# Recommender kernel: TensorE's fills in threes, two accumulator banks in turn, gathers paced one by one

## The chip, the cores and the metric

The kernel runs on one core of one Trainium2 chip. The metric is device time in microseconds. TensorE's granted clock is given as a share of 2.4 GHz; it stands at 1.00 in all windows of the steady part.

## The reference

An xDeepFM over 2048 samples, 26 sparse fields with embeddings of 32 numbers, 13 dense features, all in float32:

```
emb = tables[feat_idx, sparse]                       # 2048 x 26 x 32
linear_out = lin_sparse_w[feat_idx, sparse].sum(-1) + dense @ lin_dense_w
x0 = xk = emb; res = []
for w, bb in ((conv1_w, conv1_b), (conv2_w, conv2_b)):
    hp = einsum('bhd,bmd->bhmd', xk, x0).reshape(-1, h * 26, 32)
    xn = sigmoid(einsum('oi,bid->bod', w, hp) + bb)  # 128 outputs
    xk = xn[:, :64]; res.append(xn[:, 64:])
cin_out = concat(res).sum(-1) @ cin_w + cin_b
h1, h2, h3 = three tanh layers of 1024, 512, 256 on [emb, dense]
result = linear_out + cin_out + h3 @ deep_w + deep_b + bias
```

## The kernel before

The batch is cut into 16 tiles of 128 samples. A tile is worked on in 4 steps of 8 embedding dimensions, so that a step has 8 x 128 = 1024 columns; there are 64 steps. Tile 0, tiles 1 to 13 (a hardware loop), tile 14 and tile 15 are four copies of one program (`over_tiles`; `ahead` is 3, 2, 1, 0). After them the three dense layers run over 4 groups of 512 samples.

In one step:

- **First layer.** TensorE writes sums of two fields into PSUM (K fills, `spread_sum`, L738, 3 of 2 matmuls each), ScalarE squares them (L922) into `sq`, and TensorE contracts `sq` with weights (`contract_k`, L745) in two chunks of 512 columns. Both chunks use the one bank `xn`. ScalarE reads each chunk with three sigmoids (`read_xn`, L926 to L928) and so makes `xk` of the next step.
- **Second layer.** 13 products, number n = 0 to 12: VectorE multiplies the rows of two fields, spread over 128 partitions, with `xk` (L692). For 7 of the 13 (`BY_DMA`) two DMAs of 256 KB each copy the field's rows from DRAM into a buffer `xb` (SyncE, L471). For 6 (`BY_PE`) TensorE spreads them into PSUM (`spread_pair`, L731); the six take three slots of PSUM (`bc`) in turn together with the K fills. One spread is two matmuls of 32 rows, on row groups that depend on `group_of(n)`. TensorE contracts each product into bank `y2` (L751, 4 matmul records for a product, two at a time on the two halves of the columns), and ScalarE reads it (L932).
- **Next tile.** GpSimd gathers 26 rows for each sample with 26 indirect DMAs (L542). In one step of a tile (`deep_step`: step 1, in tile 0 step 2) TensorE turns the gathered tile (D fills, L723), ScalarE copies it twice (L918, L919), VectorE takes the remainder (`lower_deep`, L658), and SyncE dumps both to DRAM (`dump`, L420; `dump_halves`, L433), from where `x0t` is loaded on ScalarE's queue (`load_rows`, L370).
- GpSimd also adds up what ScalarE has read (`add_up`, L553 to L558).

`STEP_WORK` is the order on TensorE, and ScalarE follows it: "of_last" are products of the step before, "of_this" those of this step, "first" is a chunk of the first layer. VectorE takes the products in order of n. SyncE loads `xb` again once TensorE has contracted it.

Of the kernel before, what the change touches and what calls it, by code (L numbers as in the profile page):

```python
# [41 lines left out]
def second_of_pair(p):  # L42
# [12 lines left out]
ORDER = [0, 1, 2, 3, 8, 4, 5, 9, 6, 7, 10, 11, 12]  # L55
BY_PE = (3, 4, 6, 7, 9, 10)
# [8 lines left out]
    ("of_last", (8, 9, 10)),  # L65
    ("fill", (("D", 0), ("D", 1), ("D", 2))),
    ("of_last", (11, 12)),
    ("fill", (3, 4)),
    ("first", 0),
    ("of_this", (0, 1, 2)),  # L70
    ("fill", (6, 7)),
    ("first", 1),
    ("fill", (9, 10)),
    ("of_this", (3, 4, 5, 6, 7)),
# [40 lines left out]
assert all(group_of(BY_PE[i]) != group_of(BY_PE[i + 1]) for i in range(0, len(BY_PE), 2))  # L115
# [17 lines left out]

AHEAD = 5, 12, 19
assert AHEAD[-1] <= M

# [19 lines left out]
def build(nc, table, sparse, dense_t, lin_dense, pair_a, pair_b, diag_ab, w2rows, conv1_b, conv2_b,  # L158
          cin_w, scalars, W1, b1, W2, b2, W3, b3, deep_w, select, ident_f, out):
    with ExitStack() as ctx:  # L160
# [81 lines left out]
        xn = pb("xn", [P, CHUNK])  # L242
        y2 = pb("y2", [P, CHUNK])
# [78 lines left out]
        def k_contracted_by(s, c):  # L322
            return s * 2 + (2 + c + 1)

# [51 lines left out]
        def _(sp):  # L376
# [96 lines left out]
            def tile(t, is_first, ahead):  # L473
                for sl in range(STEPS):
                    s = t * STEPS + sl
                    for i, n in enumerate(BY_DMA):
                        if not (is_first and sl == 0):
                            sp.wait_ge(contracted, contracted_by(s - 1, n))
                            hold()
                        spread_by_dma(t, sl, i)  # L480
                        if i == 2 and sl == 2 and not is_first and ahead > 0:
                            dump_halves(t + 1)
                    if sl == 2 and is_first:
                        dump_halves(t + 1)
                    if sl == deep_step(ahead) and ahead > 0:
                        dump(t + 1)
                    if sl == STEPS - 1 and ahead == 0:
                        sp.wait_ge(dense_dumped, 64)
                        load_x(0, 0, 1)
# [36 lines left out]
        def _(pool):  # L526
# [43 lines left out]

            def tile(t, is_first, ahead):
                s = t * STEPS
                if is_first:
                    free_emb(t, DEEP_N)
                    gather(range(PAIRS), gathered)
                else:
                    if ahead > 0:
                        gather(range(AHEAD[2], AHEAD[2] + 3), gathered)
                    add_up(t - 1, STEPS - 1, r2, r2_step, y2_read, 1, sum2)
                    if ahead > 0:  # L580
                        gather(range(AHEAD[2] + 3, M), gathered)
                add_up(t, 1, r1, r1_step, xn_read, 2, sum1)
                if is_first:
                    gather(range(PAIRS, M), gathered)
                elif ahead > 1:
                    free_emb(t + 1, filled_by(t, 1, ("D", DEEP_N - 1), ahead))
                    gather(range(AHEAD[0]), gathered)
                add_up(t, 2, r1, r1_step, xn_read, 2, sum1)
                if is_first:
                    add_up(t, 1, r2, r2_step, y2_read, 1, sum2)  # L590
                    free_emb(t + 1, filled_by(t, 2, ("D", DEEP_N - 1), ahead))
                    gather(range(9), gathered)
                else:
                    if ahead > 1:
                        gather(range(AHEAD[0], AHEAD[0] + 3), gathered)
                    add_up(t, 1, r2, r2_step, y2_read, 1, sum2)
                    if ahead > 1:
                        gather(range(AHEAD[0] + 3, AHEAD[1]), gathered)
                add_up(t, 3, r1, r1_step, xn_read, 2, sum1)
                if is_first:  # L600
                    gather(range(9, 13), gathered)
                elif ahead > 1:
                    gather(range(AHEAD[1], AHEAD[1] + 3), gathered)
                add_up(t, 2, r2, r2_step, y2_read, 1, sum2)
                if is_first:
                    gather(range(13, AHEAD[2]), gathered)
                elif ahead > 1:
                    gather(range(AHEAD[1] + 3, AHEAD[2]), gathered)
# [5 lines left out]
        def _(dve):  # L614
# [61 lines left out]
            def tile(t, is_first, ahead):  # L676
                for sl in range(STEPS):
                    s = t * STEPS + sl
                    start = is_first and sl == 0
                    for n in range(PAIRS):  # L680
                        if n == 0:
# [11 lines left out]
                        if n == 3 and sl == deep_step(ahead) and ahead > 0:  # L693
                            dve.wait_ge(gathered, t * GATHERED + GATHERED)
                            sum_linear(t + 1)
                        if n == 5 and sl == deep_step(ahead) and ahead > 0:
                            dve.wait_ge(deep_rounded, t * DEEP_N + 2 * DEEP_N)
                            for ks in DEEP_PARTS:
                                lower_deep(ks)
# [18 lines left out]
        def _(pe):  # L718
# [23 lines left out]
            def contract_k(c):  # L742
                cols = slice(c * CHUNK, (c + 1) * CHUNK)
                for k in range(K1):
                    last = nc.tensor.matmul(xn[:, :], w1s[:, k, :], sq[k][:, cols], start=(k == 0), stop=(k == K1 - 1))  # L745
                last.then_inc(k_contracted, 1)

            def contract(n):
                src = product(n)
                for c in range(2):  # L750
                    last = nc.tensor.matmul(y2[H * c:H * c + H, :], w2s[:, ORDER[n], :], src[:, c * CHUNK:(c + 1) * CHUNK],  # L751
# [43 lines left out]
            contract_k(0)  # L795
            pe.wait_ge(xn_read, 1)
            contract_k(1)
# [3 lines left out]
            def add_term(w, x, start=False, stop=False):  # L801
                for g in range(GROUPS):
                    last = nc.tensor.matmul(xn[32 * g:32 * g + 1, 0:CHUNK], w, x[:, g * CHUNK:(g + 1) * CHUNK],
# [3 lines left out]
            def add_linear():  # L807
                for c in range(CHUNK // P):
                    for g in range(GROUPS):
                        t = g * (CHUNK // P) + c  # L810
                        nc.tensor.matmul(xn[32 * g:32 * g + 1, c * P:(c + 1) * P], lin_sum[:, t:t + 1], idf[:, :],
                                         start=False, stop=False, skip_group_check=True)

            def tile(t, is_first, ahead):
                for sl in range(STEPS):
# [4 lines left out]
                    for kind, what in STEP_WORK:  # L820
# [268 lines left out]
```

## Time and profile before

| | |
|---|---|
| median of 3 runs | 1616.76 us (1615.88 to 1619.33) |
| the profiled execution's own time | 1624.22 us |
| its span | 1622.4 us |
| TensorE, share of the span | 95% |
| VectorE / ScalarE / GpSimd | 68% / 40% / 44% |
| DMA queue of SyncE / ScalarE / GpSimd | 75.0% / 4.1% / 3.8% of 16 engines |

A line of the profile gives an engine's busy time, the number of instructions, and, in the chain of waits, what released each piece of work. "Idle before" is the time an engine had nothing to do before a group, with the work that ended it. Step 0 of a tile is the first of its four.

### The profile page before, as it was taken

The numbers are of one execution on the slowest core, as the hardware profiler recorded it, in microseconds if no ns is written. First come the engines' busy times: TensorE is split into PE (matmuls) and PEld (weight loads), VectorE is DVE, ScalarE is ACT, GpSimd is POOL, SyncE is SP. The second block draws the span as 40 slices with busy tenths as digits, with TensorE's granted clock in tenths as the row PEclk, the third lists the DMA queues.
The fourth block names the chain that finished last, engine by engine and source line by source line (L and its number), as shares of the span: only waits on it lengthen the run. The fifth ranks groups of instructions, "written<-read, shape, count | busy, mean of one in ns | idle before, by whom it ended". The sixth has DMA issues, their size and how long they took to land.

```text
span 1622.4 us, 23599 instructions
## 1 busy us (share of the span) xinstructions
PE 1543.6 (95%) x6584; PEld 656.8 (40%) x6584; DVE 1104.7 (68%) x1017; ACT 643.5 (40%) x904; POOL 709.2 (44%) x600
## 2 busy tenths in 40 slices
PE   0598999999999999999999999999999999999999
PEld 0232333333333333333333333333333336787876
DVE  3276777777777877787777777787877783333332
ACT  2342434344434443434443434434343323344443
POOL 7356565556555556565555646464731110000000
PEclk9899999999999999999999999999999999999999
DMA  6688999999999999999998989898999884634531
GB/s 126 143 183 194 231 214 223 217 231 209 226 212 225 211 224 209 221 214 229 210 228 200 232 201 231 201 240 201 237 203 235 204 210 122 186 120 147 175 104 53
DMA packets 178599, 319.80 MB, mean 197 GB/s; under 512 B 31132, under 2 KB 106812, under 8 KB 178524
## 3 DMA queue, kind: packets, MB, share of 16 engines
q1 hardware_dynamic: 155423, 298.87, 75.0%
q10 hardware_dynamic: 9828, 13.43, 4.1%
q0 software_dynamic: 13312, 7.06, 3.8%
q8 instruction: 19, 0.31, 0.1%
q14 instruction: 17, 0.14, 0.0%
HBM read 297.93 MB, written 21.31 MB: 197 GB/s over the span
## 4 chain that ended last, share of the span: by engine, by line
PE 86%; issue 4%; DVE 3%; another core or an unknown queue 2%; POOL 2%; DMA 1%; SPq 1%; ACT 1%; ACTq 0%; DVEq 0%; POOLq 0%
PE y L751 42%; PE xn L745 19%; PE bc L880 16%; PE bc L731 5%; PE bc L738 3%; DVE hp L692 2%; POOL emb L542 2%; PE bc L723 1%; DVE xb L692 1%; SPq L465 1%; DMA x0t<-x_halves 1%; DMA x_lo<-dense_halves 0%; ACTq L370 0%; DMA emb<-table,idx_stage 0%
## 5 line engine op out<-in xcount | busy, mean ns | idle before, releaser
L692 DVE TENSOR_TENSOR hp<-bc,xk 128x1024 f32<-128x1024 f32 x384 | 453.9, 1219 | 271.3 <-PE bc L731 136.0
L542 POOL DMA_INDIRECT emb<-table,idx_stage x416 | 515.9, 1240 | 145.5 <-issue 126.3
L692 DVE TENSOR_TENSOR xb<-xb,xk 128x1024 f32<-128x1024 f32 x448 | 546.5, 1264 | 27.9 <-ACT xk L927 23.9
L751 PE MATMUL y<-xb,w2s 128*64 128x512 f32 x1792 | 436.0, 601 | 0.0
L745 PE MATMUL xn<-sq,w1s 128*128 128x512 f32 x768 | 369.7, 618 | 4.4 <-issue 4.4
L751 PE MATMUL y<-hp,w2s 128*64 128x512 f32 x1536 | 366.0, 597 | 0.0
L553 POOL TENSOR_TENSOR r<-r 128x512 f32<-128x512 f32 x96 | 123.5, 1287 | 351.0 <-ACT r L932 181.3
L926 ACT ACTIVATE xk<-xn,bias 64x512 f32<-64x512 f32 x128 | 87.4, 683 | 438.5 <-PE xn L745 248.8
L922 ACT ACTIVATE sq<-bc 128x1024 f32<-128x1024 f32 x192 | 182.9, 1026 | 197.5 <-PE bc L738 145.8
L751 PEld LDWEIGHTS y<-xb,w2s 128*64 128x64 f32 x1792 | 116.0, 136 | 248.8 <-issue 201.5
L745 PEld LDWEIGHTS xn<-sq,w1s 128*128 128x128 f32 x768 | 137.5, 192 | 162.6 <-issue 154.8
L751 PEld LDWEIGHTS y<-hp,w2s 128*64 128x64 f32 x1536 | 104.8, 137 | 199.5 <-issue 172.4
L713 DVE TENSOR_TENSOR h_lo<-h_raw,h_hi 128x512 fp32r<-128x512 f32 x48 | 33.2, 692 | 154.2 <-ACT h_hi L1021 154.2
L731 PE MATMUL bc<-x0t,sel 32*128 32x512 f32 x768 | 97.2, 496 | 6.8 <-DVE hp L692 3.5
L731 PEld LDWEIGHTS bc<-x0t,sel 32*128 32x128 f32 x768 | 36.8, 182 | 158.1 <-issue 122.0
L932 ACT ACTIVATE r<-y,bias 128x512 f32<-128x512 f32 x64 | 44.0, 687 | 127.4 <-PE y L751 127.4
L880 PE MATMUL bc<-x_hi,w_hi 128*128 128x512 f32 (+1 forms) x224 | 88.4, 395 | 3.6 <-DMA x_lo<-dense_halves 2.8
L1019 ACT ACTIVATE h_raw<-bc,bd 128x512 f32<-128x512 f32 x48 | 33.0, 688 | 142.7 <-PE bc L880 142.7
L928 ACT ACTIVATE r<-xn,bias 64x512 f32<-64x512 f32 x128 | 87.5, 684 | 3.2
L880 PE MATMUL bc<-x_lo,w_hi 128*128 128x512 f32 (+1 forms) x224 | 88.2, 394 | 0.0
L880 PE MATMUL bc<-x_hi,w_lo 128*128 128x512 f32 (+1 forms) x224 | 88.1, 394 | 0.0
L927 ACT ACTIVATE xk<-xn,bias 64x512 f32<-64x512 f32 x128 | 87.2, 681 | 1.7
(57 smaller groups left out, 843.3 us busy)
## 6 DMA issues: line engine op xcount, KB each, us to landing
xb<-x_rows SPq DMA_DIRECT2D x896, 256.0 KB
w_raw<-W SPq DMA_DIRECT2D x32, 448.0 KB
x0t<-x_halves ACTq DMA_DIRECT2D x252, 52.0 KB
x_halves<-deep_halves SPq DMA_DIRECT2D x30, 384.0 KB
w_raw<-W SPq DMA_DIRECT2D x16, 512.0 KB
emb<-table,idx_stage POOLq DMA_INDIRECT x416
x_hi<-x_halves SPq DMA_DIRECT2D x24, 256.0 KB
x_lo<-x_halves SPq DMA_DIRECT2D x24, 256.0 KB
```

The lines of the kernel that those rows point to most:

```text
L542: nc.gpsimd.indirect_dma_start(out=emb[:, m, :], out_offset=None, in_=table, in_offset=bass.IndirectOffsetOnAxis(ap=idx_stage[:, m:m + 1], ...
L553: nc.gpsimd.tensor_tensor(total, r[:, 0, :] if sl == 1 else total, r[:, sl, :], ALU.add).then_inc(step, 1)
L692: nc.vector.tensor_tensor(product(n)[:, :], x[:, :], xk[sl % 2][:, :], ALU.mult).then_inc(multiplied, 1)
L731: last = nc.tensor.matmul(bc[slot][:, c * CHUNK:(c + 1) * CHUNK], sel[rows, ORDER[n], :], x[rows, :], start=True, stop=True)
L738: last = nc.tensor.matmul(bc[slot][:, c * CHUNK:(c + 1) * CHUNK], sel[rows, PAIRS + k, :], x[rows, :], start=True, stop=True)
L745: last = nc.tensor.matmul(xn[:, :], w1s[:, k, :], sq[k][:, cols], start=(k == 0), stop=(k == K1 - 1))
L751: last = nc.tensor.matmul(y2[H * c:H * c + H, :], w2s[:, ORDER[n], :], src[:, c * CHUNK:(c + 1) * CHUNK], start=(n == 0), stop=(n == PAIRS ...
L880: last = nc.tensor.matmul(bc[a % 2][:, 0:CHUNK], w[a % 2][part, k, :], x[part, at, :], start=(k == 0 and i == 0), stop=(k == rows - 1 and ...
L922: nc.scalar.activation(sq[k][:, :], bc[slot][:, :], ACT.Square).then_inc(squared, 1)
L926: nc.scalar.activation(xk[slot][0:H, cols], xn[0:H, :], ACT.Sigmoid, bias=bias1[0:H, :])
L927: nc.scalar.activation(xk[slot][H:P, cols], xn[0:H, :], ACT.Sigmoid, bias=bias1[0:H, :]).then_inc(xk_made, 1)
L928: nc.scalar.activation(r1[H * c:H * c + H, sl, :], xn[H:P, :], ACT.Sigmoid, bias=bias1[H:P, :]).then_inc(xn_read, 1)
```

## The change

1. `ORDER` and `BY_PE`: TensorE spreads products 0, 1, 2 and 5, 6, 7, in two fills of three; 3, 4 and 8 to 12 are copied by DMA.
2. `STEP_WORK`: products 5 to 12 are contracted a step later, 0 to 4 in their own step. The two chunks of the first layer stand next to each other. The last step has an order of its own (`FINAL_WORK`).
3. Two banks `acc` take turns: chunk c of step sl goes to `acc[(sl + c) % 2]`, the products to `acc[sl % 2]`.
4. Each gather waits until a named product is multiplied (`gather_in`).
5. VectorE does the tile's sum and remainders ahead of product 0 instead of behind products 3 and 5.
6. SyncE dumps the halves right before the rows, and the inputs of the first dense group are loaded in steps of tiles 14 and 15 instead of at the end.

```diff
-ORDER = [0, 1, 2, 3, 8, 4, 5, 9, 6, 7, 10, 11, 12]
-BY_PE = (3, 4, 6, 7, 9, 10)
+ORDER = [0, 8, 1, 3, 4, 9, 2, 10, 5, 6, 7, 11, 12]
+BY_PE = (0, 1, 2, 5, 6, 7)
...
+FINAL_WORK = (
+    ("fill", (0, 1, 2)),
+    ("of_last", (5, 6, 7, 8, 9, 10, 11, 12)),
+    ("fill", (5, 6, 7)),
+    ("of_this", (0, 1)),
+    ("terms", None),
+    ("of_this", (2, 3, 4)),
+)
...
-        xn = pb("xn", [P, CHUNK])
-        y2 = pb("y2", [P, CHUNK])
+        acc = [pb(f"acc{i}", [P, CHUNK]) for i in range(2)]
+        terms = acc[(STEPS - 2) % 2]
...
+        def first_acc(sl, c):
+            return acc[(sl + c) % 2]
...
-                        if i == 2 and sl == 2 and not is_first and ahead > 0:
-                            dump_halves(t + 1)
-                    if sl == 2 and is_first:
+                    if sl == deep_step(ahead) and ahead > 0:
                         dump_halves(t + 1)
-                    if sl == deep_step(ahead) and ahead > 0:
                         dump(t + 1)
-                    if sl == STEPS - 1 and ahead == 0:
-                        sp.wait_ge(dense_dumped, 64)
-                        load_x(0, 0, 1)
+                    if ahead == 1:
+                        if sl == 0:
+                            sp.wait_ge(dense_dumped, 64)
+                        load_x(0, sl, 4 * STEPS)
+                    if ahead == 0 and sl < STEPS - 1:
+                        load_x(0, 1 + sl, STEPS)
...
+            def gather_in(s, fields, ns):
+                for m, n in zip(fields, ns):
+                    pool.wait_ge(multiplied, multiplied_by(s, n))
+                    hold()
+                    gather((m,), gathered)
...
+                if ahead > 0:
+                    gather_in(s - 1, range(20, 23), (8, 10, 12))
+                add_up(t - 1, STEPS - 1, r2, r2_step, y2_read, 1, sum2)
+                if ahead > 0:
+                    gather_in(s, range(23, M), (2, 4, 6))
+                add_up(t, 1, r1, r1_step, xn_read, 2, sum1)
...
                     for n in range(PAIRS):
+                        if n == 0 and sl == deep_step(ahead) and ahead > 0:
+                            dve.wait_ge(gathered, t * GATHERED + GATHERED)
+                            sum_linear(t + 1)
+                            for i, ks in enumerate(DEEP_PARTS):
+                                dve.wait_ge(deep_rounded, t * DEEP_N + (DEEP_N + i + 1))
+                                lower_deep(ks)
...
                             for use in uses:
-                                if is_product(use):
+                                if not is_d(use):
                                     slot_free(t, sl, use, is_first, ahead)
...
                         elif kind == "of_this":
-                            if what[0] == 0 and not start:
-                                pe.wait_ge(y2_read, s)
+                            if what[0] == 0:
+                                pe.wait_ge(xn_read, s * 2 + (2 if final else 3))
...
                         elif kind == "first" and not final:
                             if what == 0:
                                 pe.wait_ge(squared, squared_by(s, K1 - 1))
-                            pe.wait_ge(xn_read, s * 2 + (2 + what))
-                            contract_k(what)
+                            if what == 0:
+                                pe.wait_ge(xn_read, s * 2 + 2)
+                            elif not start:
+                                pe.wait_ge(y2_read, s)
+                            contract_k(what, first_acc(sl, what))
```

What TensorE runs in one step, from the K fills of a step on, before the change (`bc` are the three slots, `x0t` the rows, `hp` and `xb` the products, a K fill has `L738`, a spread `L731`; a product has 2 matmuls here):

```order
L738 MATMUL bc<-x0t,sel 128x512 x6
L751 MATMUL y<-xb,w2s 64x512 x2
L751 MATMUL y<-hp,w2s 64x512 x4
L751 MATMUL y<-xb,w2s 64x512 x4
L731 MATMUL bc<-x0t,sel 128x512 x4
L745 MATMUL xn<-sq,w1s 128x512 x3
L751 MATMUL y<-xb,w2s 64x512 x6
L731 MATMUL bc<-x0t,sel 128x512 x4
L745 MATMUL xn<-sq,w1s 128x512 x3
L731 MATMUL bc<-x0t,sel 128x512 x4
L751 MATMUL y<-hp,w2s 64x512 x4
```

and the same place after it:

```order
L755 MATMUL bc<-x0t,sel 128x512 x6
L768 MATMUL acc<-hp,w2s 64x512 x6
L768 MATMUL acc<-xb,w2s 64x512 x10
L748 MATMUL bc<-x0t,sel 128x512 x6
L762 MATMUL acc<-sq,w1s 128x512 x6
L748 MATMUL bc<-x0t,sel 128x512 x6
L768 MATMUL acc<-hp,w2s 64x512 x6
L768 MATMUL acc<-xb,w2s 64x512 x4
```

The two chunks of the first layer moved together, the spreads went from three blocks of two to two blocks of three, and eight products of the step before stand in a row behind the K fills where there were five.

GpSimd at the start of the loop's tile, before (each DMA is the gather of one field):

```order
L542 DMA emb<-table,idx_stage 128x33 x3
L553 TENSOR_TENSOR r<-r 128x512 [waits r2_step]
L556 TENSOR_TENSOR r<-r 128x256 [waits r2_step]
L558 TENSOR_TENSOR sum<-r 128x128
L542 DMA emb<-table,idx_stage 128x33 x4
```

and after, where tile 14 has the same order without the register work:

```order
L550 DMA emb<-table,idx_stage 128x33 [waits multiplied] x3
L561 TENSOR_TENSOR r2<-r2 128x512 [waits r2_step,y2_read]
L564 TENSOR_TENSOR r2<-r2 128x256 [waits r2_step]
L566 TENSOR_TENSOR sum2<-r2 128x128 [waits r2_step]
L550 DMA emb<-table,idx_stage 128x33 [waits multiplied] x3
```

Each gather has got a wait for VectorE, and the last of the 26 (the third of the lower group) waits for product 6 of step 0.

## Rows read from the trace of the kernel before

**Rows 1.** The page, busy time of each engine.
```profile
PE 1543.6 (95%) x6584; PEld 656.8 (40%) x6584; DVE 1104.7 (68%) x1017; ACT 643.5 (40%) x904; POOL 709.2 (44%) x600
```

**Rows 2.** Chain of waits, 231 to 272 us: start, length, work.
```profile
231.83 4.44 PE y L751 x20
236.28 0.89 PE bc L738 x3
237.16 4.45 PE y L751 x20
241.61 0.44 PE bc L731 x3
242.05 2.77 PE xn L745 x6
244.82 2.73 PE y L751 x12
...
251.20 4.44 PE y L751 x20
...
259.26 0.92 PE bc L723 x7
...
271.61 0.58 PE y L751
```

**Rows 3.** TensorE in order of time: start, length, line, tiles, idle time before.
```profile
136.19 1.65 PE L738 MATMUL bc<-x0t,sel 64*128 64x512 f32 x6 [7.42 <-DMA x0t<-x_halves]
...
1302.61 0.97 PE L738 MATMUL bc<-x0t,sel 64*128 64x512 f32 x6
...
1321.88 1.03 PE L751 MATMUL y<-xb,w2s 128*64 128x512 f32 x4
...
1342.01 1.89 PE L751 MATMUL y<-xb,w2s 128*64 128x512 f32 x8
1346.70 0.47 PE L880 MATMUL bc<-x_hi,w_hi 128*128 128x512 f32 x1 [2.80 <-DMA x_lo<-dense_halves]
```

**Rows 4.** VectorE in order of time, same step as rows 2.
```profile
242.20 2.35 DVE L692 TENSOR_TENSOR hp<-bc,xk 128x1024 f32<-128x1024 f32 x2 [2.01 <-PE bc L731]
```

**Rows 5.** ScalarE in order of time, same step (ACTq: DMAs it issues).
```profile
241.81 3.58 ACTq L370 DMA_DIRECT2D x0t<-x_halves  x4
245.58 0.68 ACT L926 ACTIVATE xk<-xn,bias 64x512 f32<-64x512 f32 x1 [3.23 <-PE xn L745]
246.28 0.68 ACT L927 ACTIVATE xk<-xn,bias 64x512 f32<-64x512 f32 x1
246.99 0.68 ACT L928 ACTIVATE r<-xn,bias 64x512 f32<-64x512 f32 x1
```

**Rows 6.** GpSimd, a gather at 611.55 us, and GpSimd's DMA queue from 614.5 to 615.4.
```profile
611.55 1.70 POOL L542 DMA_INDIRECT emb<-table,idx_stage  x1 [0.22 <-issue]
...
q0 software_dynamic: 31, 0.02, 20.4%
```

**Rows 7.** GpSimd, a tile's last gather, its DMA queue from 413.5 to 414.3, TensorE's D fills.
```profile
406.92 0.95 POOL L542 DMA_INDIRECT emb<-table,idx_stage  x1 [0.31 <-issue]
...
q0 software_dynamic: 2, 0.00, 0.8%
...
416.19 0.98 PE L723 MATMUL bc<-idf,emb 128*128 128x128 f32 x7
```

**Rows 8.** ScalarE's DMA issues at 597.45 us, and its DMA queue from 601.2 to 606.
```profile
597.45 3.58 ACTq L370 DMA_DIRECT2D x0t<-x_halves  x4
...
q10 hardware_dynamic: 156, 0.21, 22.2%
```

**Rows 9.** Busy time by stretch, 400 to 600 us; last: TensorE's clock, DMA share, GB/s.
```profile
400.00:600.00 200.00, 198.97 (x846) 68.86 (x844) 157.26 (x145) 82.27 (x118) 112.32 (x94) 1.00 0.95 220
```

**Rows 10.** Tile 0, SyncE's dump of the halves and ScalarE's load behind it.
```profile
120.04 0.99 SPq L433 DMA_DIRECT2D x_halves<-deep_halves  x2
...
125.25 3.20 ACTq L370 DMA_DIRECT2D x0t<-x_halves  x4
```

**Rows 11.** VectorE, the remainder of the second dense weights.
```profile
1348.47 1.09 DVE L664 TENSOR_TENSOR w_lo<-w_raw,w_hi 128x896 fp32r<-128x896 f32 x1 [8.29 <-ACT w_hi L909]
```

## Prediction before the run

> **What bounds the kernel now.** I read the page first: TensorE is busy for 95% of the span, VectorE for 68%, and nothing else over half [rows 1]. Then the chain of waits over two steps of a middle tile. It holds nothing but TensorE: blocks that follow each other without a gap, 19.37 us from one block of products (231.83) to the same block a step later (251.20), and 20.41 us (251.20 to 271.61) in the step that turns the next tile [rows 2]. So TensorE's own order is the bound, and the reader should see two things in it. First, a block costs more than its matmuls: products take 4.44 us for 20 records and 2.73 for 12 [rows 2], so a record costs (4.44 - 2.73) / 8 = 0.214 us and a block 0.165 us on top. The first layer's records run one at a time where the products' run in twos, so I take 2 x 0.214 = 0.428 for one; six make 2.57, and the block's 2.77 leaves 0.20. Second, waits are rare: from the K fills of tile 0's step 3 (136.19) to those of tile 15's step 2 (1302.61) are 59 steps, 14 of them with D fills, and 1166.4 us [rows 3]. Without any wait they would be 59 x 19.37 + 14 x 1.04 = 1157.4. So 9 us are waits and a slow restart at 136.
>
> **The steps, summed.** Before, a step is three blocks of products (4.44, 4.45, 2.73), K fills 0.89, three fills of two spreads at 0.44, two blocks of the first layer at 2.77 [rows 2]: 19.37. After, it is K fills 0.89, products 5 to 12 in one block (32 records: 0.165 + 32 x 0.214 = 7.01), two fills of three spreads, one block of the first layer (12 x 0.428 + 0.20 = 5.34), products 0 to 4 (4.44). The one unknown is the fill of three spreads. Their groups alternate: two can run on different rows of the array, the third needs the rows of the first. The rows give 0.44 for one round (two spreads) and 0.89 for three rounds (K fills, which use all rows each) [rows 2], so a further round costs (0.89 - 0.44) / 2 = 0.225, and three spreads are two rounds: 0.665. The ends are 0.44 (all at once) and 0.89 (each alone). With 0.665 the step is 0.89 + 7.01 + 0.665 + 5.34 + 0.665 + 4.44 = 19.01, which is 0.36 less. Over 59 steps: -21.2. At the ends: -48 and +5. I take the middle, since the groups are known. In a D step the D fills cut the block of products in two, before and after alike, so the 1.04 stays.
> The Trainium skill (TensorE: Matmul & The Clock Gate, Part 3, The mechanism) says that a weight load runs beside a matmul in flight only when the row group differs. By that rule the third spread waits for the first, as in the 0.665. Were its weights kept waiting for the whole array, the fill would be the 0.89 and the step 19.46.
>
> **Do the others keep up?** I walk through a step, with 0 as the start of the fill of 0, 1, 2 (B). VectorE starts 0.6 after such a fill begins and then makes a product every 1.13 us (2.35 for two) [rows 4]: products 0 to 4 end at 1.8, 3.0, 4.1, 5.2, 6.4. TensorE's first layer ends at 6.0, and its fill of 5, 6, 7 needs the slots of 0, 1, 2, free at 4.1: no wait. Product 5 ends at 7.9, 6 at 9.0, 7 at 10.1, 12 at 15.8. TensorE contracts 0 to 4 from 6.7 to 11.1. The K fills, which now wait for product 7 (10.1), start at 11.1; product 12 is needed at 18.1. ScalarE issues four loads from 0.2 on and starts to read chunk 0 at 4.0, as it does now (245.58 against 241.61), done at 6.1 [rows 2, 5]; TensorE needs that bank at 6.7. This wait, which is new, has the least room, 0.5 us. Behind it stand all contractions of the step. Chunk 1 is read from 6.1 to 8.2, far before the next step needs `xk`. ScalarE's squares end at 14.9, needed at 19. So none of the new waits should end last, and 5 of the 9 us of waits before go, since slots are free 0.9 to 1.9 us ahead; the other 4 (the restart mostly) stay. Ends: 0 and -9.
>
> **DMA.** The engines are busy for 0.95 of a stretch of steps at 220 GB/s [rows 9]; the bytes stay and the steps get 2% shorter, which asks for 224. The copies' room grows: product 3's buffer is asked for at -8.9 and needed at 5.2; that of 8 at -3.4, needed at 11.2; that of 12 at about 2.4 (SyncE issues one behind the other), needed at 14.7. The loads of `x0t` lose room: issued until 3.8, they are needed at 11.1, where before it was 255.64, 14.0 after B. In the rows all their packets fall before 606, within 5.0 us of the last issue's end (601.03) [rows 8]; 7.3 are left. I take 0.
> The Trainium skill (DMA: Bandwidth & Descriptors, Queues, rings and completion order) says that a DMA engine goes round its queues packet by packet, so that these loads don't stand behind five queued copies. The row with 156 packets of ScalarE's queue amid SyncE's agrees; in a strict order of issue they would come some 4 us later and just in time. Neither changes the sum.
>
> **The gathers.** The last one now waits for product 6 of step 0, at 9.0, and is issued at 9.15. The D fills stand at 11.1 + 0.9 + 2.7 = 14.7. That leaves 5.5 us where a last gather now has 9.3 (406.92 to 416.19) [rows 7]. How long does one take? From its start to its packets' end 3.8 us for one after a pause [rows 6], 7.2 for the last of a burst (406.92 to after 413.5, a few packets) [rows 7], and some time more until it is counted, which no row shows. So TensorE waits 0 to 2 us for each of 14 tiles: 0 to +28. Paced gathers are nearer to the first row; I take 0.45 each: +6. With that wait VectorE's remainder and the dumps move too, but they have 2 us of room.
>
> **Tile 0.** Step 3 waits for the load of `x0t` behind the dump: dump at 120.04, load at 125.25, K fills at 136.19 after 7.4 us idle [rows 3, 10]. The remainders now stand ahead of product 0, so the dump can leave earlier, but the load is needed earlier too and the chain (10.9 us from load to fills) remains; it sets when tile 1 starts, so what the prologue saves is lost in it. I take -2, ends -6 and +4.
>
> **The end.** The last step has three more products to contract than before (8 of the old step instead of 5), of which the step before had fewer: 23.3 us from its first block to its end (0.67 fills + 7.0 + 0.6 wait for product 2 + 0.67 + 1.8 + terms 2.9 + 2.7 + 6.9), against 21.8 (1321.88 to 1342.01 + 8 x 0.214 = 1343.7) [rows 3]: +1.5. The dense layers' input is there by then: the 3.0 us from 1343.7 to 1346.70 shrink to 0.3 [rows 3], but the second dense product, 5.1 us behind, needs weights that come 5.8 us after the end (1349.56) [rows 11], through ScalarE, which waits for GpSimd's last sums: -2.7 + 0.7 = -2.0. The loads of 4 MB now lie in the steps of tile 15, 1 MB each, where gathers and dumps are absent; I cost them at 0, and up to +4 if the copies fall behind.
>
> **Sum.** -21.2 - 5 + 6 - 2 + 1.5 - 2.0 = -22.7 us. The profiled execution took 1624.22, so 1601.5; it lay 7.5 above the median of 1616.76, from which the forecast is counted: **1594 us**.
>
> **Rivals.**
> 1. *Gathers land late (slower).* Place: TensorE before the D fills. Saved without this term: 28.7 us; over 14 tiles that is gone at a wait of 2.05 us each, thus at 7.6 us from the gather's start to its count. At 9.3 us, the most that the trace allows (it never waited), the wait is 3.8 x 14 = 53 and the time 1641. For it: 7.2 in rows 7, and DMA at 0.95. Against it: 3.8 in rows 6, and the burst is gone. Typical of it: 1630.
> 2. *A fill of three costs what the K fills cost.* Step 19.46: +0.45 x 59 = 26.5 over the forecast, 1620. For it: nothing in the trace shows three spreads. Against: two go at once at 0.44.
> 3. *DMA can't go faster.* If 220 GB/s is its limit, a step falls behind the copies and stays near 19.3: 1610. For it: the share of 0.95. Against: TensorE does not wait for copies now [rows 2].
> 4. *All waits go.* No gather wait, all 9 us go: 1584.
> 5. *The turn of banks or the adjacent chunks make ScalarE's read the last* (0.5 us of room missed by 0.3): +18, 1612.
>
> **Chances.** Forecast 0.56, rival 1 0.08, rival 2 0.06, rival 3 0.08, rival 4 0.15, rival 5 0.07. The range that holds 8 in 10 takes in rivals 4, 3 and part of 5: 1580 to 1612. A difference under 0.2% (3.2 us) can't be told from none here. Faster by more than that: forecast, 4, 3, 5 and little else, 0.85; same 0.05 (rival 2 in part); slower 0.10.
>
> **What would show it.** Right: in the chain of waits a step of 19.0 us with blocks of 32 and 20 records; a fill of three at 0.66 to 0.67; the first layer in one block of 5.3. K to K over the same 59 steps near 1142. Wrong: fills of 0.89; TensorE idle before its D fills for gathers by more than 1 us a tile, or before the first product of a step for ScalarE's reads of the first layer's bank; a share of DMA at 1.0 with VectorE waiting for `xb`; the time from the last product to the first dense matmul still near 3.

## The result: slower by half a per cent

| | before | changed |
|---|---|---|
| median, us (lowest to highest, 16 runs each, one chip) | 1617.62 (1613.85 to 1619.61) | 1625.80 (1616.50 to 1632.06) |
| ratio, 95% interval | | 1.0051 (1.0040 to 1.0063) |
| profiled execution: its time, its span | 1624.22, 1622.4 | 1626.34, 1624.5 |

A second measurement on another chip gave 1626.18 against 1616.67, ratio 1.0062 (1.0046 to 1.0077). Forecast were 1594 us and a range of 1580 to 1612: the sign is wrong and the range missed.

The changed kernel's page, busy time by engine, the chain's shares by engine, and the groups of the K fills and of VectorE's products from copies:
```profile
PE 1523.4 (94%) x6584; PEld 669.6 (41%) x6584; DVE 1125.6 (69%) x1017; ACT 643.7 (40%) x904; POOL 679.7 (42%) x600
...
PE 61%; DMA 25%; ACTq 7%; issue 3%; POOL 2%; ACT 1%; SPq 1%; DVE 0%; POOLq 0%; DVEq 0%
...
L716 DVE TENSOR_TENSOR xb<-xb,xk 128x1024 f32<-128x1024 f32 x448 | 563.1, 1314 | 3.4 <-DMA xb<-x_rows 3.3
...
L755 PE MATMUL bc<-x0t,sel 64*128 64x512 f32 x384 | 63.8, 437 | 48.3 <-DMA x0t<-x_halves 38.9
```
TensorE is busy for 20.2 us less than before [rows 1] and the span is no shorter: the saving is there and has been handed back as waiting. Who is waited for stands in the second and the last line: a quarter of the chain is DMA, and the K fills sat idle for 48.3 us, mostly for the loads of `x0t`.

The chain of waits over two steps of the stretch of [rows 2], changed kernel (start, length, what):
```profile
225.68 8.43 DMA x0t<-x_halves
...
234.15 0.96 PE bc L755 x6
235.12 7.02 PE acc L768 x32
242.13 0.66 PE bc L748 x6
242.79 5.35 PE acc L762 x12
248.14 0.66 PE bc L748 x6
248.80 4.44 PE acc L768 x20
253.25 0.89 PE bc L755 x6
254.14 2.73 PE acc L768 x12
256.86 0.92 PE bc L740 x7
257.78 4.44 PE acc L768 x20
```
Two things are to be seen. Where nothing is late, a step is 0.89 + 7.02 + 0.66 + 5.35 + 0.66 + 4.44 = 19.02 us, against 19.01 forecast, and each block is within 0.01 of its term. And in front of it stands a load that took 8.43 us from the start of its issue (225.68) until TensorE could go on, 7.66 from the issue's end (226.45). The waits, first in the whole run, then from 180 to 1300 us (who <- for whom: us, times, longest):
```profile
PE bc L755 <- DMA x0t<-x_halves: 38.9, 41, 8.6
```
```profile
PE bc L755 <- DMA x0t<-x_halves: 29.1, 38, 2.2
```
Outside tile 0 they are short, 0.8 us on average (29.1 / 38), but two steps in three have one. TensorE's own rows, beside [rows 3]:
```profile
130.09 1.65 PE L755 MATMUL bc<-x0t,sel 64*128 64x512 f32 x6 [8.62 <-DMA x0t<-x_halves]
...
213.14 1.62 PE L755 MATMUL bc<-x0t,sel 64*128 64x512 f32 x6 [2.22 <-DMA x0t<-x_halves]
...
1304.71 0.96 PE L755 MATMUL bc<-x0t,sel 64*128 64x512 f32 x6
...
1346.71 1.08 PE L768 MATMUL acc<-xb,w2s 128*64 128x512 f32 x4 [0.16 <-DVE xb L716]
1347.72 0.50 PE L899 MATMUL bc<-x_hi,w_hi 128*128 128x512 f32 x1
```
The 59 steps take 1304.71 - 130.09 = 1174.6 us, where [rows 3] give 1166.4. By its blocks they should take 59 x 19.02 + 14 x 1.04 = 1136.7. Of the 37.9 that are left, 29.5 are listed as waits for loads (38.9 without the two in tile 0, 8.6 and 0.7). Some 4.0 are slower matmuls behind the two longest waits: the K fills at 213.14, after 2.22 us idle, took 1.62 where those at 1304.71 took 0.96, and the step from 130.09 lasted until 151.41, 2.3 us over its blocks without a wait in it; that from 213.14 lost 1.7 in the same way. TensorE's granted clock was down there (us, busy time of PE, PEld, DVE, ACT, POOL; then clock, DMA share, GB/s):
```profile
130.00:134.00 4.00, 3.91 (x12) 1.66 (x14) 0.00 (x0) 2.85 (x3) 3.26 (x5) 0.50 0.04 4
...
213.00:216.00 3.00, 2.86 (x10) 1.33 (x12) 2.60 (x3) 2.06 (x3) 2.67 (x2) 0.53 1.02 231
```
0.50 is the lower of its two levels, 1.2 GHz. From 217 us on it stood at 1.00, so the shorter waits behind it did not slow the matmuls. The last 4.4 us have no single cause; the kernel with later K fills below, which has no waits for loads in its steps, has some 2.7 of the same kind. The profiled pair adds up: steps +8.2, tile 0 6.1 earlier, the dense stage's start 1.1 nearer to the last K fills and the rest 1.1 longer (0.8 of it TensorE's waits for the second dense weights, 1.5 against 0.7), in all +2.1, the two spans' difference. Before's profiled execution lay 6.6 above its median and the changed one's 0.5, so the medians differ by 8.2.

### The profile page after: what moved, and what is told of

Same layout as the page of the kernel before. It is cut to its first block, busy times and chain, and to the rows that moved or that the text cites. A ratio compares the mean times of both kernels' runs of the same rounds, so it can differ in the third digit from the quotient of the medians.

```text
span 1624.5 us, 24360 instructions
## 1 busy us (share of the span) xinstructions
PE 1523.4 (94%) x6584; PEld 669.6 (41%) x6584; DVE 1125.6 (69%) x1017; ACT 643.7 (40%) x904; POOL 679.7 (42%) x600
## 4 chain that ended last, share of the span: by engine, by line
PE 61%; DMA 25%; ACTq 7%; issue 3%; POOL 2%; ACT 1%; SPq 1%; DVE 0%; POOLq 0%; DVEq 0%
PE acc L768 32%; DMA x0t<-x_halves 24%; PE bc L899 16%; ACTq L377 7%; PE acc L762 7%; PE bc L755 4%; POOL emb L550 2%; PE bc L748 2%; PE bc L740 1%; DMA xb<-x_rows 1%; SPq L478 1%; DMA x_halves<-deep_halves 1%; ACT sq L941 0%; ACT r L952 0%; DMA emb<-table,idx_stage 0%
## 5 line engine op out<-in xcount | busy, mean ns | idle before, releaser
L768 PE MATMUL acc<-xb,w2s 128*64 128x512 f32 x1792 | 407.2, 593 | 0.2 <-DVE xb L716 0.2
L768 PE MATMUL acc<-hp,w2s 128*64 128x512 f32 x1536 | 360.4, 604 | 0.0
L762 PE MATMUL acc<-sq,w1s 128*128 128x512 f32 x768 | 351.3, 607 | 2.2 <-ACT sq L941 2.2
L768 PEld LDWEIGHTS acc<-xb,w2s 128*64 128x64 f32 x1792 | 127.2, 137 | 250.6 <-issue 230.2
L762 PEld LDWEIGHTS acc<-sq,w1s 128*128 128x128 f32 x768 | 142.4, 192 | 182.2 <-issue 182.2
L768 PEld LDWEIGHTS acc<-hp,w2s 128*64 128x64 f32 x1536 | 99.5, 137 | 196.0 <-issue 160.1
L946 ACT ACTIVATE xk<-acc,bias 64x512 f32<-64x512 f32 x128 | 87.5, 684 | 227.8 <-PE acc L762 112.3
L952 ACT ACTIVATE r<-acc,bias 128x512 f32<-128x512 f32 x64 | 44.0, 687 | 288.0 <-PE acc L768 288.0
L755 PE MATMUL bc<-x0t,sel 64*128 64x512 f32 x384 | 63.8, 437 | 48.3 <-DMA x0t<-x_halves 38.9
L948 ACT ACTIVATE r<-acc,bias 64x512 f32<-64x512 f32 x128 | 87.6, 684 | 3.2
L947 ACT ACTIVATE xk<-acc,bias 64x512 f32<-64x512 f32 x128 | 87.3, 682 | 1.6
```

Source lines behind the costliest of these rows:

```text
L755: last = nc.tensor.matmul(bc[slot][:, c * CHUNK:(c + 1) * CHUNK], sel[rows, PAIRS + k, :], x[rows, :], start=True, stop=True)
L762: last = nc.tensor.matmul(acc_k[:, :], w1s[:, k, :], sq[k][:, cols], start=(k == 0), stop=(k == K1 - 1))
L768: last = nc.tensor.matmul(acc_y[H * c:H * c + H, :], w2s[:, ORDER[n], :], src[:, c * CHUNK:(c + 1) * CHUNK], start=(n == 0), stop=(n == PA ...
L946: nc.scalar.activation(xk[slot][0:H, cols], xn[0:H, :], ACT.Sigmoid, bias=bias1[0:H, :])
L948: nc.scalar.activation(r1[H * c:H * c + H, sl, :], xn[H:P, :], ACT.Sigmoid, bias=bias1[H:P, :]).then_inc(xn_read, 1)
```

## Why the loads are late

The DMA queues in two stretches, changed kernel, 242.4 to 245.9 and 245.9 to 252.1 us (q1 holds SyncE's copies, q10 ScalarE's loads; packets, MB, share of 16 engines):
```profile
q1 hardware_dynamic: 245, 0.80, 101.5%
```
```profile
q1 hardware_dynamic: 368, 1.20, 87.3%
q10 hardware_dynamic: 156, 0.21, 17.7%
```
And before, 241.5 to 245.5, the same place of its step:
```profile
q1 hardware_dynamic: 243, 0.79, 67.2%
q10 hardware_dynamic: 46, 0.07, 9.5%
```
ScalarE's issues, and the first reads of the shared bank, changed kernel:
```profile
242.34 3.58 ACTq L377 DMA_DIRECT2D x0t<-x_halves  x4
246.10 0.68 ACT L946 ACTIVATE xk<-acc,bias 64x512 f32<-64x512 f32 x1 [3.23 <-PE acc L762]
...
247.50 0.68 ACT L948 ACTIVATE r<-acc,bias 64x512 f32<-64x512 f32 x1
```
Before, loads issued from 241.81 [rows 5] moved 46 packets by 245.5. Now loads issued from 242.34 moved none by 245.9, while the copies' queue filled all engines; then their 156 packets ran to 252.1, 6.2 us behind the last issue's end (245.92), with K fills due at 253.25.

The late first packet alone does not tell the two kernels apart. In the step of [rows 8] all 156 packets lie behind 601.2; from 597.4 to 601.2 the kernel before moved none of its loads either:
```profile
q1 hardware_dynamic: 241, 0.79, 97.4%
q0 software_dynamic: 58, 0.03, 6.5%
```
The end of the last packet does. Taken from the packets of q10 over the 58 steps from tile 1's second K fills on, it lies behind the end of the step's last issue by 2.8 to 5.4 us in the kernel before (median 4.1) and by 5.8 to 8.4 in the changed one (median 6.7); the ranges do not meet. The first packet comes behind the start of the first issue by 2.1 to 4.2 us (median 2.5) and by 3.1 to 6.6 (4.3). Where TensorE waited, it went on 1.1 us behind the last packet on average. So with the old landing the slowest load would have been counted after 6.5 us (5.4 + 1.1), inside the 7.3 that are left; with the new one the typical load takes 7.8.

What moved is on SyncE. Products 3, 4, 8, 9, 10, 11 and 12 now come by copy, and the buffers of the last five come free in one run. From 238.9 to 246 it issues 10 DMAs, five copies, and from 246.2 to 252 none; the loads are issued beside the second half of that run, with 6 of the DMAs in the same stretch (242.3 to 246). Before, 3 stood beside them (241.8 to 245.4), 6 lay in the 7.1 us up to the end of the loads' issue (238.3 to 245.4) where there are now 10, and 6 followed until 252.

## The experiments

All are timed beside the kernel before on the same chip; its median is given, since it differs by chip. Theory: the loads of `x0t` come too late for K fills that moved from 14.0 to 11.1 us behind B (the start of the fill of 0, 1, 2), because they now lie beside a run of copies. Rivals: the paced gathers, DMA as a whole being too slow for steps of 19 us, and something dearer in the new order itself.

**Loads earlier, one part undone.** The changed kernel, ScalarE's loads issued at the K fills, in step 2 of a tile behind the squares, and not at B (tile 0 as it is). The issues of step 2 are left out here.
```diff
+ if ("K", 0) in what and not is_first and sl != 2 and ("K", 0) in there and (sl < 2 or ahead > 0):
+     for c in range(2):
+         load_rows(act, t + (sl + 2) // STEPS, (sl + 2) % STEPS, c)
...
- if what == int(late) and (sl < 2 or ahead > 0):
+ if is_first and what == int(late) and (sl < 2 or ahead > 0):
```


> The changed kernel, but ScalarE issues the loads of x0t at the K fills (before its squares) instead of behind the reading of the products, in step 2 of a tile behind the squares; tile 0 stays. The room from the last issue to TensorE's K fills grows from 7.3 us to about 15 (11 in step 2). Theory 1 (late loads are the whole loss: 34 us of waits at the K fills of steps 4 to 62 and some 4 us of slow restarts): the waits vanish outside tile 0, steps of 19.0 us, 1590 us (1584 to 1596). Theory 2 (the DMA engines, 0.95 busy, are the limit of the step): the wait moves to VectorE's copies or to the gathers, steps stay near 19.7, above 1612.

1600.20 us against 1628.60, ratio 0.9843 (0.9817 to 0.9869). K fills wait for loads twice, in tile 0 (131 us) and in the first step behind it (153 us), whose loads are still issued in tile 0:
```profile
PE bc L755 <- DMA x0t<-x_halves: 10.3, 2, 9.3
```
In all later steps the waits are gone as expected, but 1600.20 is above the 1584 to 1596 that I gave. The profiled execution took 1596.38, 6.2 more than that of the kernel with later K fills below. Its 59 steps take 1143.8 us against 1142.0 there, although three D fills wait for gathers in them (3.6 us), and most of the rest lies in tile 0, whose wait for the load is 9.3 against 5.8. What puts the median another 4 us higher no trace shows.

**A quarter of each copy.** Outside tile 0 the copies bring 256 of 1024 columns, so the products of the others are computed from old data; order and timing of issues stay.
```diff
- spread_by_dma(t, sl, i)
+ spread_by_dma(t, sl, i, COLS if is_first else COLS // 4)
```


> The changed kernel, but outside tile 0 each copy for xb brings only a quarter of its columns (the products of the rest use old numbers), so that SyncE's queue moves a quarter of its bytes in as many packets; ScalarE's loads and their room stay. Theory 1 with queueing (a load lands late because it shares the DMA engines with five copies): packets of a load end within 4 us of the last issue, no waits at the K fills, 1588 us. If a load's 7 to 9 us are its own (issue, small rows in DRAM), the waits stay and so do 1625 us.

1593.62 against 1628.60, ratio 0.9784 (0.9760 to 0.9808). The two waits that are left stand in the same two places (132 and 154 us):
```profile
PE bc L755 <- DMA x0t<-x_halves: 11.0, 2, 9.5
```
So with the same room and the same order the loads are in time when the copies carry less: their last packet ends 1.3 to 3.3 us behind the last issue's end (median 1.7). This run alone can't tell a crowded moment from DMA that is too slow as a whole, since all copies got lighter; the later K fills below can.

**Gathers as before, in bursts.**
```diff
- for m, n in zip(fields, ns):
-     pool.wait_ge(multiplied, multiplied_by(s, n))
-     hold()
-     gather((m,), gathered)
+ gather(fields, gathered)
```


> The changed kernel with the gathers in bursts (no wait for a product before each, else in the same places). Theory 1: the gathers are 4% of the DMA engines' time; the waits at the K fills move by little, 1625 us plus or minus 5. Theory 3 (the pacing is what hurts, since it puts a gather's packets between those of the loads in every step): the K fills' waits of steps 0 and 1 and 3 fall by half or more, 1608 us.

1635.71 against 1628.60, ratio 1.0042 (1.0024 to 1.0059), in the span of the changed kernel's own two ratios, 1.0051 and 1.0062. The waits are the changed kernel's:
```profile
PE bc L752 <- DMA x0t<-x_halves: 38.4, 41, 8.6
```
Undoing the pace wins nothing back, so it is not the cause. In microseconds the run is 10 above the changed kernel on its two chips; since that kernel was not timed on this chip, whether the bursts cost something here stays open.

**K fills later.** Instead of moving the loads, their use: products 5, 6, 7 are contracted ahead of the K fills, 8 to 10 behind them. Waits on the K fills' slots, then already met, are dropped.
```diff
-    ("fill", (("K", 0), ("K", 1), ("K", 2))),
     ("of_last", (5, 6, 7)),
+    ("fill", (("K", 0), ("K", 1), ("K", 2))),
+    ("of_last", (8, 9, 10)),
     ("fill", (("D", 0), ("D", 1), ("D", 2))),
-    ("of_last", (8, 9, 10, 11, 12)),
+    ("of_last", (11, 12)),
```


> The changed kernel with the K fills behind products 5, 6, 7 of the step before instead of ahead of them (D fills behind 8, 9, 10), ScalarE's issues as they are. The room of the loads grows from 7.3 to 9.9 us, what the kernel before had. Theory 1: no or few waits at the K fills (loads land 7 to 9 us after the last issue, counted a little later, so some of 0.5 us may stay), 1592 us (1586 to 1602). Theory 2: above 1612.

1590.17 against 1628.60, ratio 0.9767 (0.9747 to 0.9788). Its chain holds only TensorE, here from a fill of 0, 1, 2 (third row from the end) back; and its one wait for a load is tile 0's:
```profile
240.64 7.02 PE acc L769 x32
247.66 0.90 PE bc L756 x6
248.56 2.73 PE acc L769 x12
251.28 0.92 PE bc L741 x7
252.20 1.87 PE acc L769 x8
254.07 0.66 PE bc L749 x4
254.73 5.35 PE acc L763 x12
260.07 0.66 PE bc L749 x4
```
```profile
PE bc L756 <- DMA x0t<-x_halves: 5.8, 1, 5.8
```
The K fills stand 0.66 + 5.35 + 0.66 + 7.02 = 13.7 us behind B, close to the old 14.0, with all copies whole and in the new order. Repeated on a third chip, with nothing changed:

> The kernel with the later K fills once more, to stand beside the next two and to tell chips apart: 1590 us (1587 to 1594), since nothing in its steps waits for a DMA.

1589.10 against 1616.52, ratio 0.9831 (0.9814 to 0.9847). Against the changed kernel's 1625.80 that is 37 us. By the profiled executions (spans 1624.5 and 1588.2) the 59 steps take 1142.0 us in place of 1174.6, so 32.6 of the 36.3 us lie there: this is what the waits for loads and the slower matmuls behind them cost in the steps. The other 3.7 lie in tile 0. The copies are issued as before this edit and the loads' last packets come as late as in the changed kernel, 5.5 to 8.8 us behind the last issue's end (median 6.7); what changed is that 9.9 us are there for them.

**The changed kernel once more.**

> The changed kernel as it is, so that it stands beside the other runs of this call. Both theories: slower than the kernel before by 0.2% to 0.7%, waits for x0t at the K fills 30 us and more outside tile 0.

1626.18 against 1616.67, ratio 1.0062 (1.0046 to 1.0077); 47 waits of K fills for loads, 39.9 us.

**Less room in the old order.** The kernel before, its loads always issued behind the reading of the first chunk. They then end their issue at 235.23 and TensorE starts K fills at 242.10, a room of 6.9 us, less than the changed kernel's 7.3.
```diff
- late = is_first and sl == 2
+ late = True
```


> The kernel before with one edit: ScalarE issues the loads of x0t behind the reading of chunk 0, at about 5.5 to 9.1 us of the step instead of 0.2 to 3.8, so that 4.9 us are left until the K fills instead of 10.4. Order, banks, copies and gathers are those of before. Theory 1 (room decides, and it is too small below some 7 us): waits for x0t at most K fills, 0.5 to 2 us each, +30 to +90 us. If only the five queued copies of the new order make a load late, the waits stay under 0.3 us each and the time within +10 us.

1634.01 against 1616.67, ratio 1.0096 (1.0079 to 1.0113).
```profile
PE bc L738 <- DMA x0t<-x_halves: 21.0, 13, 8.2
```
Of these 21.0, 8.2 are tile 0's. Summed over TensorE's rows, steps 0 to 2 of the later tiles have 2.2, where the changed kernel has 17.7; step 3, whose loads lie beside the dump of the halves, has 10.6 (11.8). The loads' last packets end 3.4 to 7.3 us behind the last issue's end, median 4.8. So scarce room alone costs little in most steps while the copies are spread out; the run of copies makes it dear. Neither branch of the expectation came out: it had 4.9 us of room where 6.9 are there, and the measured +17.3 lies between its +10 and its +30. The span is 11.9 us longer than before's: 6.8 in the 59 steps (1173.2), 2.1 in tile 0, and 3.0 behind the last K fills, where TensorE's granted clock fell to 0.50 from 1355 to 1362 us, behind 3.0 us idle before the first dense matmul; in the kernel before it stayed at 1.00 behind 2.8 us idle.

**Tile 0's dump earlier**, added to the kernel with later K fills: halves are dumped behind the copies of product 4.
```diff
+ if is_first and i == 1 and sl == deep_step(ahead):
+     dump_halves(t + 1)
...
- dump_halves(t + 1)
+ if not is_first:
+     dump_halves(t + 1)
```


> The kernel with the later K fills, and in tile 0 SyncE dumps the halves of tile 1 behind the copies of product 4 instead of behind those of 12. Theory: the wait in tile 0's step 3 (6 to 9 us, the load behind the dump behind the copies) shrinks by 3 to 6 us: 3 to 6 us below the run with later K fills alone (1590), 1586. If the load waits for its own DMA only, no change.

1585.34 against 1616.67, ratio 0.9811 (0.9797 to 0.9825).
```profile
125.96 0.96 PE L759 MATMUL bc<-x0t,sel 64*128 64x512 f32 x6 [3.83 <-DMA x0t<-x_halves]
```
Tile 0's last K fills start 1.0 us earlier than in the run with the dump as it was on this chip (126.93, the run with the input late below), and take 0.96 in place of 1.65. The granted clock falls just behind them instead (0.64 from 126 to 129 us): the next 20 records take 6.18 us, as against 4.46 later on. The slow restart is not gone. Again on the third chip:

> The kernel with later K fills and the early dump of tile 0 once more, beside the two above: 1585 us (1582 to 1589).

1586.20 against 1616.52, ratio 0.9814 (0.9797 to 0.9830). Beside the later K fills alone on this chip (1589.10, 1587.20 to 1589.87; here 1582.80 to 1587.31) the earlier dump is worth some 3 us, the lower end of the 3 to 6 expected; the K fills start at 123.44 against 126.97. This version beats both kernels.

**The dense layers' input late**, as before, in the kernel with later K fills.
```diff
- if ahead == 1:
-     if sl == 0:
-         sp.wait_ge(dense_dumped, 64)
-     load_x(0, sl, 4 * STEPS)
- if ahead == 0 and sl < STEPS - 1:
-     load_x(0, 1 + sl, STEPS)
+ if sl == STEPS - 1 and ahead == 0:
+     sp.wait_ge(dense_dumped, 64)
+     load_x(0, 0, 1)
```


> The kernel with the later K fills, but the inputs of the first dense group are loaded in the last step, as before the change. Theory of the forecast (early loads are worth 2 us net, as the second dense product waits for weights at 5.8 us anyway): +2 to +3 us against 1590, with TensorE idle for about 3 us ahead of the first dense matmul.

1597.84 against 1616.67, ratio 0.9879 (0.9864 to 0.9895). First dense matmuls:
```profile
1317.45 0.77 PE L897 MATMUL bc<-x_hi,w_hi 128*128 128x512 f32 x1 [8.97 <-DMA x_lo<-dense_halves]
1318.01 0.63 PE L897 MATMUL bc<-x_hi,w_lo 128*128 128x512 f32 x1
...
1317.00:1319.00 2.00, 1.55 (x4) 1.30 (x5) 0.00 (x0) 0.00 (x0) 0.00 (x0) 0.50 0.33 127
```
9 us idle, then matmuls of 0.63 in place of 0.39, with the granted clock at 0.50 (last line, a stretch as above). By the ratios (0.9879 against 0.9831) the early loads are worth 8 us; I had 2.0. Late loads cost 9 here and 2.8 before [rows 3] because SyncE gets to them later: it issues the 16 loads from 1295.5 to 1312.8, until 4.3 us behind the end of TensorE's last product (1308.5), and in the kernel before from 1328.0 to 1342.1, 1.6 us ahead of it (1343.7).

**Bursts where there is room**, on the version with the earlier dump.

> The kernel with later K fills and the early dump of tile 0, gathers in bursts. Where x0t has room, the pacing should be worth nothing by theory 1 (last gather of a tile then starts earlier, D fills never wait): 1585 us plus or minus 3. If the pacing has a worth of its own (bursts delay copies or loads by more than the 9.9 us of room): above 1590 us.

1585.64 against 1616.52, ratio 0.9811 (0.9795 to 0.9828): the pace is worth nothing there either.

**Chunks apart**, the same version with the fill of 5, 6, 7 between the two chunks of the first layer.
```diff
     ("first", 0),
+    ("fill", (5, 6, 7)),
     ("first", 1),
-    ("fill", (5, 6, 7)),
```


> The kernel with later K fills and the early dump of tile 0, but the spreads of products 5, 6, 7 stand between the two chunks of the first layer. Theory of the block's own cost (0.20 us for a block of the first layer beside its matmuls): two blocks of 2.77 instead of one of 5.35, steps of 19.2 us, 12 us slower: 1597 us. If adjacency costs or brings nothing: 1585 us.

1641.75 against 1616.52, ratio 1.0158 (1.0139 to 1.0177); TensorE's rows:
```profile
255.49 2.84 PE L766 MATMUL acc<-sq,w1s 128*128 128x512 f32 x6
259.01 0.72 PE L752 MATMUL bc<-x0t,sel 32*128 32x512 f32 x6 [0.67 <-DVE hp L720]
259.66 2.84 PE L766 MATMUL acc<-sq,w1s 128*128 128x512 f32 x6
```
A step is 20.0 us, not the 19.2 that I expected from the block's cost alone, and the time is 45 us over the 1597 expected. The fill needs the slots of 0, 1 and 2, and VectorE takes longer for three products than one chunk does: in 63 steps TensorE waits 43.6 us for it there. So adjacent chunks are worth 1.0 us a step: 0.2 for the block and most of the other 0.8 for work that covers VectorE.

## Why the prediction was wrong, by its own steps

- **The step that failed**: "The loads of `x0t` lose room: ... 7.3 are left. I take 0." The landing time, 5.0 us, was read from [rows 8], with the old spacing of the copies, and set against a need in the new one. I had worked out the copies' new times in the sentence before, rightly (8 at -3.4, 12 at 2.4; issued from -3.2 to 3.9), and did not carry them into the loads' time. With the changed order their packets end 5.8 to 8.4 us behind the last issue, and TensorE goes on 1.1 us later. The next paragraph allowed for some 4 us more and called that just in time; by its own figures, 5.0 + 4 against 7.3, it was not. Measured, the term is 29.5 us of waits in the steps, and 32.6 with what follows them (1174.6 against 1142.0). The earlier loads, the lighter copies and the later K fills each remove them in all steps that they touch. It was not among the rivals either, and rival 3 (DMA can't go faster) fell too: at the same bytes steps of 19.0 us run throughout.
- The sentence from the Trainium skill (DMA: Bandwidth & Descriptors, Queues, rings and completion order) that an engine goes round its queues packet by packet did not protect the loads: here no packet of theirs moved in the 3.5 us behind their first issue. No run here tests the rule itself.
- **The steps' sum** was right: 19.02 against 19.01, the fill of three 0.66 against 0.665. Rival 2 (0.89) is out.
- **ScalarE's read** of the shared bank was right: it ends at 248.2, TensorE's products start at 248.80, room 0.6. Rival 5 is out.
- **The gathers** (+6): mis-sized, 0. A tile's last one in this stretch:
```profile
251.87 0.95 POOL L550 DMA_INDIRECT emb<-table,idx_stage  x1 [1.64 <-DVE hp L716]
```
  It starts 9.7 us behind B (242.13), 0.6 later than forecast, and the D fills at 256.86 wait for nothing: it was counted within 5.0 us. Behind tile 0 no D fill of the changed kernel or of the one with later K fills waits for a gather; the kernel with the loads earlier has three such waits, 3.6 us. The K fills were on time in this step (253.25, 11.1 behind B), so rival 1 is out on its own merits.
- **Tile 0** (-2): mis-sized, -6.1 (136.19 to 130.09), the end of the range that I gave. That is one pair of executions; a second profile of the changed kernel has 128.60.
- **The end**: the last step's length (+1.5) was near, 23.8 against 23.3; VectorE waited for copies there, which I had at 0:
```profile
1345.43 1.23 DVE L716 TENSOR_TENSOR xb<-xb,xk 128x1024 f32<-128x1024 f32 x1 [1.23 <-DMA xb<-x_rows]
```
  The dense layer then starts at once, as said.
- **Waits** (-5 of 9): apart from the loads', none are left in the steps, so rival 4's mechanism was right. With the loads in time the forecast would have been some 4 us too high: the kernel with later K fills takes 1589 and 1590. Its 59 steps take 1142.0 us, the number that I gave for K to K; but my terms add up to 1166.4 - 21.2 - 5 + 6 = 1146, so that this is the sum without most of the 6 for the gathers.

## What to carry to other kernels

When an order is changed, list every transfer whose issue or need moves, and take its landing time at the queue that it will meet, not at the one of the trace. A transfer with 2 us of room by an old landing time has none if a run of large copies now stands beside it. Where room is short, moving the use (three products here) costs nothing and gained 37 us, 33 of them in the steps; and what looks like a saving of one block can be worth five times that if the longer block covers another engine.

## What was not expected of the hardware

- Beside a run of five copies (10 DMAs in 7 us) on one queue, small loads on another ended 5.8 to 8.4 us after their last issue; with the copies spread out, 2.8 to 5.4; beside copies of a quarter of the bytes, 1.3 to 3.3. Whether the depth of the queue or the bytes in flight decide is not separated.
- The kernel before takes 1628.6, 1616.7 and 1616.5 us on three chips, a spread of 0.7%, where the kernel with later K fills takes 1590.2 and 1589.1. So a ratio to before carries the chip with it (or the time of the measurement: each chip was used at one time only).
- TensorE's granted clock fell from 1.00 to 0.50 behind some idle times and not behind others of like length: behind 2.2 us it fell (changed kernel, 213 us), behind 2.8 us it did not (kernel before, 1346 us), behind 3.0 us it did (old order with late loads, 1355 us). So the price of a wait is not its length alone.
- The gathers' pace slows VectorE. Its products from copies take 1306 to 1317 ns in the kernels with paced gathers and the chunks together, and 1250 in the two with bursts. The page's row for the version with room, in bursts and paced:
```profile
L717 DVE TENSOR_TENSOR xb<-xb,xk 128x1024 f32<-128x1024 f32 x448 | 534.6, 1250 | 4.6 <-DMA xb<-x_rows 4.4
```
```profile
L720 DVE TENSOR_TENSOR xb<-xb,xk 128x1024 f32<-128x1024 f32 x448 | 564.8, 1317 | 4.4 <-DMA xb<-x_rows 4.3
```
  These are 30 us of VectorE's time, and nothing of the kernel's, since TensorE does not wait for it. Which part of GpSimd's work meets the products stays open.
